# First convolution in float16 parts, its padding on ScalarE and GpSimd, pair loops written out

## What is computed

```python
x = x + L0(gn(x))   # a 3x3 convolution whose weights are mixed for each image
x = x + L1(gn(x))   # 3x3 convolution by groups, quantised weights and sums
x = x + L2(gn(x))   # a two-dimensional cosine transform of each 28x28 plane
x = x + L3(gn(x))   # attention over 784 tokens, 4 heads

def L0(x):
    pooled = mean(x, axis=(2, 3))
    y = (relu(pooled @ fc1_w.T) @ fc2_w.T + fc2_b).reshape(B, 4, 64)
    prob = softmax(y / 4, axis=1)
    agg_w = einsum('bko,koihw->boihw', prob, weight)   # 64x64x3x3 per image
    return conv3x3(x, agg_w)                           # padding 1
```

## Time and profile before

| | us |
|---|---|
| median of 3 runs | 1765.08 (1764.5 to 1770.01) |
| the profiled execution, its own time | 1766.6 |
| its span in the profile | 1763.9 |
| busy: PE / DVE / ACT / POOL | 1597.4 / 1292.2 / 1023.8 / 455.2 |

### The profile page before, as it was taken

How to read it: one execution, slowest core, us unless ns; L and a number is a source line. 1 busy time by engine, 2 the same in 40 slices (tenths; PEclk the granted TensorE clock), 3 DMA queues, 4 the chain that set the end, 5 groups by cost and what they waited for, 6 DMA issues and landing times.

```text
span 1763.9 us, 30283 instructions
## 1 busy us (share of the span) xinstructions
PE 1597.4 (91%) x10848; PEld 730.4 (41%) x10848; DVE 1292.2 (73%) x2666; ACT 1023.8 (58%) x1401; POOL 455.2 (26%) x364
## 2 busy tenths in 40 slices
PE   0699869999686799999999999999999999999997
PEld 0333335555575234444344444444444444444332
DVE  5677557887787687787677777877778778777762
ACT  0000156676132157777677777777777777777676
POOL 0400011110300313234233242333333423333212
PEclk9999989999897689999999999999999999999999
DMA  8122166665000423322333234323332343233300
GB/s 204 32 53 52 31 96 108 108 100 92 1 0 1 64 33 50 50 43 35 52 50 50 44 41 63 49 34 50 51 52 44 40 63 50 34 52 50 52 12 19
DMA packets 71213, 92.82 MB, mean 53 GB/s; under 512 B 23516, under 2 KB 64340, under 8 KB 70960
## 3 DMA queue, kind: packets, MB, share of 16 engines
q1 hardware_dynamic: 67728, 89.59, 31.3%
q0 software_dynamic: 3360, 1.61, 1.3%
HBM read 9.00 MB, written 6.42 MB: 9 GB/s over the span
## 4 chain that ended last, share of the span: by engine, by line
PE 76%; DVE 10%; DMA 5%; ACT 3%; SPq 3%; issue 2%; POOL 1%; DVEq 0%; ACTq 0%
PE ps L1050 19%; PE ps L1040 16%; PE ps L985 14%; PE ps L860 8%; PE ps L884 5%; DVE arena L1430 3%; PE ps L899 3%; DMA arena<-arena 3%; PE ps L1006 2%; ACT arena L678 2%; PE ps L946 2%; DMA x<-x_in 2%; SPq L431 2%; PE ps L1023 1%; PE ps L1014 1%
## 5 line engine op out<-in xcount | busy, mean ns | idle before, releaser
L1430 DVE TENSOR_REDUCE arena<-ps 128x1 f32<-128x392 f32 x1600 | 826.4, 561 | 258.5 <-PE ps L985 246.8
L791 ACT ACTIVATE arena<-ps 112x784 f32<-112x784 f32 x896 | 704.2, 822 | 232.2 <-PE ps L1040 224.9
L985 PE MATMUL ps<-arena 112*128 112x392 bf16 x1536 | 483.8, 341 | 16.2 <-DMA arena<-arena 8.2
L1040 PE MATMUL ps<-arena 114*112 114x392 bf16 x1792 | 443.3, 334 | 6.6 <-ACT arena L791 5.9
L1050 PE MATMUL ps<-arena 112*32 112x392 f32 x3584 | 391.2, 508 | 0.5 <-ACT arena L791 0.5
L985 PEld LDWEIGHTS ps<-arena 112*128 112x128 bf16 x1536 | 149.3, 97 | 367.2 <-DVE arena L1430 301.7
L1040 PEld LDWEIGHTS ps<-arena 114*112 114x112 bf16 x1792 | 228.1, 133 | 107.2 <-ACT arena L791 38.8
L884 PE MATMUL ps<-arena 96*128 96x392 f16 x768 | 142.2, 336 | 22.1 <-DMA arena<-arena 16.6
L678 ACT ACTIVATE arena<-ps,magic,arena 128x784 f32<-128x784 f32 x128 | 128.2, 1005 | 37.0 <-PE ps L884 36.8
L860 PE MATMUL ps<-arena 128*64 128x392 f32 (+1 forms) x768 | 139.7, 506 | 3.9 <-DMA arena<-arena 3.9
L1050 PEld LDWEIGHTS ps<-arena 112*32 112x32 f32 x3584 | 70.7, 108 | 141.8 <-issue 140.0
(11 more groups left out here) (142 smaller groups left out, 1383.7 us busy)
## 6 DMA issues: line engine op xcount, KB each, us to landing
arena<-arena SPq DMA_DIRECT2D x504, 73.5 KB, 2.7
arena<-arena SPq DMA_DIRECT2D x256, 84.2 KB, 2.7
x<-x_in SPq DMA_DIRECT2D x8, 784.0 KB, 21.0
out<-x SPq DMA_DIRECT2D x16, 392.0 KB, 2.9
arena<-arena SPq DMA_DIRECT2D x252, 24.5 KB, 2.4
arena<-arena SPq DMA_DIRECT2D x256, 1.5 KB
arena<-arena SPq DMA_DIRECT2D x16, 225.0 KB, 3.4
arena<-arena SPq DMA_DIRECT2D x16, 224.8 KB, 2.9
```

What stands on the lines that cost most here:

```text
L791: nc.scalar.activation(probs[w % 2][:, 2 * pair:2 * pair + 2, :], two(2 * place, rows=slice(0, TT)), ACT.Exp).then_inc(s_taken, 1)
L985: last = nc.tensor.matmul(ps[:, bank, 0:CH], q[0:ROWS_L, h, it * 128:(it + 1) * 128], k[0:ROWS_L, h, c * CH:(c + 1) * CH], start=True, sto ...
L1040: last = nc.tensor.matmul(ps[0:TT, 2 * place + j, 0:CH], ks[s % 4][0:ROWS_ALL, h, jt * TT:(jt + 1) * TT], qs[s % 4][0:ROWS_ALL, h, c * CH: ...
L1430: nc.vector.tensor_reduce(mx[img % 2][:, c, v:v + 1], scores, AX.X, ALU.max).then_inc(s_mf, 1)
```

## The change

- **Products.** Weights and normalised image are each split into a high and a low float16 part. The weights' two parts lie one below the other on the 128 rows (64 input channels high, 64 low); `pads` holds the image's high and low plane, each on both halves of the partitions. For each of nine taps and each image part (k) there is one product over 128 rows, so all four terms are summed: 18 steps for each half and image, in place of 6. The mixed weights are scaled by the largest weight (`w_max`), taken back when the result is added.
- **Weights.** ACT makes the high part (`agg_high`), POOL the low part (`agg_low`), PE turns them by nine products with a float16 identity, ACT copies all 1152 columns out at once (`take_weights`).
- **Padding.** DVE's `pad` is gone. ACT writes the high plane of both images and a float32 copy `xn0` (`pad`, three instructions), POOL subtracts to get the low planes (`low0`, two instructions of 64 partitions). `pads` has three buffers.
- **Second stage's weights.** POOL's sixteen instructions on them are gone; ACT scales them after pair 1's weights (`scale_w1`, eight instructions), DVE clips and rounds them after pair 3 (`quantise_w1`, two).
- **Start.** The statistics' second half has the maximum of the weights ahead of it; two small steps (`nshift`) and one on `lmax` are added to the chain, and POOL clears its planes at the very start.
- **Loops.** `pair_steps` and DVE's loops become plain repetition over 16 pairs in all three stages, on all engines.

```diff
-        pair_w = [part([128, 3, 128]) for _ in range(2)]
-        last_w = [part([C, 3, 128]) for _ in range(2)]
+        agg_parts = [part([128, 9, 2, C], F16) for _ in range(2)]
+        tap_w = [part([128, 9, 128], F16) for _ in range(2)]
+        ident16 = part([128, 128], F16)
+        w_max = part([128, 1])
+        w_max_inv = part([128, 1])
...
-        pads = [[part([128, PAD]) for _ in range(2)] for _ in range(2)]
+        pads = [[part([128, 2, PAD], F16) for _ in range(2)] for _ in range(3)]
...
-            for p in range(4):
-                step(p, None)
-            with eng.Fori(0, PAIR_LOOP[1]) as i:
-                for j in range(2):
-                    step(4 + j, i)
-            for p in (NP - 2, NP - 1):
+            for p in range(NP):
...
+                first, second = pads[p % 3]
+                sp.wait_ge(s_pad, p + 1)
+                sp.dma_start(first[C:2 * C, :, :], first[0:C, :, :]).then_inc(s_twin[p % 3], 16)
+                sp.dma_start(second[0:C, :, :], second[C:2 * C, :, :]).then_inc(s_twin[p % 3], 16)
...
+            def low0(p):
+                pool.wait_ge(s_xn0, p + 1)
+                for im in range(2):
+                    r = slice(im * C, (im + 1) * C)
+                    inner = [pads[p % 3][im][r, k, 0:HP * WP].rearrange("p (y x) -> p y x", y=HP)[:, 1:1 + H, 1:1 + W]
+                             for k in range(2)]
+                    if im == 1:
+                        pool.wait_ge(s_pad_first, p + 1)
+                    elif p >= 1:
+                        pool.wait_ge(s_agg_parts, p)
+                    nc.gpsimd.tensor_tensor(inner[1], xn0[p % 2][r, :].rearrange("p (y x) -> p y x", y=H),
+                                            inner[0], ALU.subtract).then_inc((s_pad_first, s_pad)[im], 1)
+            def agg_low(p):
+                pool.wait_ge(s_pad, p + 1)
+                pool.wait_ge(s_agg_hi, p + 1)
+                nc.gpsimd.tensor_tensor(agg_parts[p % 2][:, :, 1, :], agg[p % 2][:, :, :], agg_parts[p % 2][:, :, 0, :],
+                                        ALU.subtract).then_inc(s_agg_parts, 1)
...
+            def pad(p):
+                if p >= 3:
+                    act.wait_ge(s_conv, 2 * (p - 2))
+                if p >= 2:
+                    act.wait_ge(s_pad, p - 1)
+                for im in range(2):
+                    r = slice(im * C, (im + 1) * C)
+                    nc.scalar.activation(
+                        pads[p % 3][im][r, 0, 0:HP * WP].rearrange("p (y x) -> p y x", y=HP)[:, 1:1 + H, 1:1 + W],
+                        x[r, p, :].rearrange("p (y x) -> p y x", y=H), ACT.Identity,
+                        bias=nshift[r, p:p + 1], scale=grstd[r, p:p + 1])
+                nc.scalar.activation(xn0[p % 2][:, :], x[:, p, :], ACT.Identity, bias=nshift[:, p:p + 1],
+                                     scale=grstd[:, p:p + 1]).then_inc(s_xn0, 1)
+            def agg_high(p):
+                act.wait_ge(s_agg, p + 1)
+                if p >= 2:
+                    act.wait_ge(s_aggt, p - 1)
+                nc.scalar.activation(agg_parts[p % 2][:, :, 0, :], agg[p % 2][:, :, :], ACT.Copy).then_inc(s_agg_hi, 1)
+            def take_weights(p):
+                act.wait_ge(s_aggt, p + 1)
+                if p >= 2:
+                    act.wait_ge(s_conv, 2 * (p - 1))
+                nc.scalar.activation(tap_w[p % 2].rearrange("p t n -> p (t n)"), weights_psum,
+                                     ACT.Copy).then_inc(s_convw, 1)
+            def scale_w1():
+                act.wait_ge(s_w1, 16)
+                for g in range(NG):
+                    for s, n0 in ((inv_sw, 0), (minus_inv_sw, 64)):
+                        a = w1_raw[:, g, :, n0:n0 + 64]
+                        last = nc.scalar.activation(a, a, ACT.Identity, bias=0.0, scale=s[0:W1_ROWS, g:g + 1])
+                last.then_inc(s_w1_scaled, 1)
             roots(0)
+            act.wait_ge(s_init, 1)
+            act.wait_ge(s_l0v, 1)
+            pad(0)
             act.wait_ge(s_l0v, 3)
             nc.scalar.activation(prob[:, :, :], logit[:, :, :], ACT.Exp).then_inc(s_l0s, 1)
-            def l0(p, i):
-                act.wait_ge(s_aggt, lin(lambda q: q + 1, p, i, 2))
-                if p >= 2:
-                    act.wait_ge(s_conv, lin(lambda q: 2 * (q - 1), p, i, 2))
-                nc.scalar.activation(pair_w[p % 2].rearrange("p y n -> p (y n)"), ps[:, 0, 0:3 * 128], ACT.Copy)
-                nc.scalar.activation(last_w[p % 2].rearrange("p y n -> p (y n)"), ps[0:C, 1, 0:3 * 128],
-                                     ACT.Copy).then_inc(s_convw, 1)
-            pair_steps(l0, act)
+            pad(1)
+            agg_high(0)
+            agg_high(1)
+            take_weights(0)
+            for p in range(NP):
+                if p + 2 < NP:
+                    pad(p + 2)
+                if p + 1 < NP:
+                    take_weights(p + 1)
+                if p == 1:
+                    scale_w1()
+                if p + 2 < NP:
+                    agg_high(p + 2)
...
             def l0_transpose(p, i):
-                pe.wait_ge(s_agg, lin(lambda q: q + 1, p, i, 2))
+                pe.wait_ge(s_agg_parts, p + 1)
                 if p >= 1:
-                    pe.wait_ge(s_convw, lin(lambda q: q, p, i, 2))
-                for y in range(3):
-                    n = slice(y * 128, (y + 1) * 128)
-                    nc.tensor.transpose(ps[:, 0, n],
-                                        agg[p % 2][:, 3 * y:3 * y + 2, :].rearrange("p t i -> p (t i)"), P("ident"))
-                    last = nc.tensor.transpose(ps[0:C, 1, n], agg[p % 2][:, 3 * y + 2, :], P("ident"))
+                    pe.wait_ge(s_convw, p)
+                for t in range(9):
+                    last = nc.tensor.matmul(weights_psum[:, t * 128:(t + 1) * 128],
+                                            agg_parts[p % 2][:, t, :, :].rearrange("p k i -> p (k i)"), ident16[:, :],
+                                            start=True, stop=True)
                 last.then_inc(s_aggt, 1)
             def l0(p, i):
                 if p == 0:
                     l0_transpose(0, None)
                 pe.wait_ge(s_convw, lin(lambda q: q + 1, p, i, 2))
-                pe.wait_ge(s_twin[p % 2], lin(lambda q: 32 * (q // 2 + 1), p, i, 2))
+                pe.wait_ge(s_twin[p % 3], 32 * (p // 3 + 1))
                 for c in range(2):
                     bank = 3 + 2 * (p % 2) + c
                     if p >= 2:
                         pe.wait_ge(s_added, lin(lambda q: 2 * (q - 2) + c + 1, p, i, 2))
-                    for single in range(2):
-                        for y in range(3):
-                            for im in range(2):
-                                rows = slice(0, C if single else 128)
-                                w = (last_w if single else pair_w)[p % 2][:, y, im * C:(im + 1) * C]
-                                at = (y + c * HC) * WP + 2 * single + im
-                                rhs = pads[p % 2][im][rows, at:at + HC * WP].rearrange(
-                                    "p (y x) -> p y x", x=WP)[:, :, 0:W]
-                                last = nc.tensor.matmul(ps[im * C:(im + 1) * C, bank, 0:CH], w, rhs,
-                                                        start=(y == 0 and not single), stop=(y == 2 and single == 1))
+                    for n in range(2 * 9):
+                        (y, dx), k = divmod(n // 2, 3), n % 2
+                        at = (y + c * HC) * WP + dx
+                        for im in range(2):
+                            rhs = pads[p % 3][im][:, k, at:at + HC * WP].rearrange(
+                                "p (y x) -> p y x", x=WP)[:, :, 0:W]
+                            last = nc.tensor.matmul(ps[im * C:(im + 1) * C, bank, 0:CH],
+                                                    tap_w[p % 2][:, n // 2, im * C:(im + 1) * C], rhs,
+                                                    start=(n == 0), stop=(n == 17))
                     last.then_inc(s_conv, 1)
...
+                if q == 2:
+                    dve.wait_ge(s_w0, 16)
+                    link(v.tensor_reduce(w_max[:, :], w0[:, :, :].rearrange("p k n -> p (k n)"), AX.X, ALU.max,
+                                         apply_absolute_value=True))
+                    link(v.tensor_scalar(w_max[:, :], w_max[:, :], 1e-30, None, ALU.max))
+                    link(v.reciprocal(w_max_inv[:, :], w_max[:, :]))
...
+            link(v.tensor_tensor(nshift[:, :], gmean[:, :], grstd[:, :], ALU.mult))
+            v.tensor_scalar(nshift[:, :], nshift[:, :], -1.0, None, ALU.mult)
...
+            link(v.tensor_scalar(lmax[:, :], lmax[:, :], w_max_inv[:, 0:1], None, ALU.mult))
...
+            def quantise_w1():
+                dve.wait_ge(s_w1_scaled, 1)
+                a = w1_raw.rearrange("p g y n -> p (g y n)")
+                link(v.tensor_scalar(a, a, 0.0, QW, ALU.max, ALU.min))
```

(13 more changed lines are left out.)

83 lines of the change are left out of this document (29 added, 54 removed).

## The result

| | before | after |
|---|---|---|
| median of 4 runs, us | 1764.79 (1761.16 to 1770.01) | 1744.1 (1740.62 to 1748.47) |
| ratio, 95% interval | | 0.9885 (0.9865 to 0.9905) |
| span of the profiled execution | 1763.9 | 1746.7 |
| busy: PE / DVE / ACT / POOL | 1597.4 / 1292.2 / 1023.8 / 455.2 | 1556.9 / 1312.5 / 1087.9 / 513.0 |
| first stage's products, from PE's timeline | 62.4 to 213.2 (150.7) | 69.8 to 200.9 (131.1) |

The kernel is 20.7 us faster. The forecast was 40.4 us, 1724.7 us, and its range ended at 1742: the time lies 2 us above it. The forecast of "faster" was right, the size wrong by half.

The account below looks back on a forecast made before the run. PE alone was taken to bound the first stage, 7.31 us a pair in place of 9.31. 32.7 us saved there plus 7.7 from third-stage loops made 40.4 us, giving 1724.7 us; range 1712 to 1742.

Parts of the forecast that it names:

- I take no cost: First stage: POOL and DVE slowing each other adds nothing; PE's 7.31 us a pair still holds, with little room.
- The rival that I gave 0.16: First stage: DVE and POOL shut each other out, about 8.0 us a pair, 11 us more, 1736 us; chance 0.16.
- The range: Whole kernel: 1712 to 1742 us, holding the forecast, shutting out, no loop gain, most of the chain rival and some mixtures.
- The products: First stage on PE: 36 double steps of 0.181 us, 6.51 us a pair; lower end 6.15.
- The transposes: First stage on PE: nine 16-bit products of 128 columns with weight loads, 0.8 us a pair (0.5 to 1.1).
- PE not fed: First stage: 162 PE instructions a pair not sustained; 11.0 us a pair, 59 us more, 1784 us; chance 0.05.
- ACT and POOL: First stage: ACT busy 4.4 us and POOL 4.5 us a pair, both under PE's 7.31.
- The second stage's weights: First stage, after pair 3: `quantise_w1` takes some 2.3 us on DVE with about 1.3 free; counted at 0.3 us.
- The head: Before the first stage's products: first product at 61.5 us against 62.43, 0.9 us less, with 0.15 for disturbance by POOL.
- The third stage: Loops written out: DVE's copies 5.25 us apart throughout, 7.7 us less.
- The second: Second stage, loops written out: nothing to gain, taken as 0, bounds -1 and +3 us.
- The sum: Whole kernel: 32.7 us from the first stage and 7.7 from the loops, 40.4 us less together.

Follow-up runs that it names:

- e5: Kernel after with POOL's `low0` left out but for one pixel set to zero: 1719.71 us, ratio 0.9744.
- e6: Kernel after with each subtraction of `low0` replaced by two memsets, which write and read nothing: 1719.95 us, ratio 0.9752.
- e2: Kernel after with each subtraction of `low0` replaced by two copies with one input each: 1731.48 us, ratio 0.9817.
- e4: Kernel after with both images' planes made in one 128-partition buffer, one ACT cast, one POOL subtraction, four transfers: 1726.90 us, ratio 0.9789.
- e9: Kernel after with the hardware loops put back in the second and third stages: 1746.18 us, ratio 0.9909.
- e11: Repeat run of the kernel after with the hardware loops put back in the second and third stages: 1748.17 us, ratio 0.9907.
- e8: Kernel after with both images' planes in one buffer, the mix's first product on ACT, and first weights taken out earlier: 1720.11 us, ratio 0.9764.
- e1: Kernel after, unchanged, run once more: 1745.45 us, ratio 0.9898.

## Why the prediction was wrong

**The step that failed** is "I take no cost", for POOL and DVE slowing each other. The rival that I gave 0.16 was the truth: it said 8.0 us a pair, measured are 8.27. Its price was put at 11 us against the forecast's 7.31 a pair; against what PE really allows, 6.84, it cost 19.4 us of PE's waiting (e5 and e6 against after: 131.1 - 111.6 = 19.5). The rival's mechanism is what the traces show, its nearness in part luck: its sum put POOL's 4.5 us and the mix into one time, while POOL is busy 12.0 of 20 us and the pair is DVE's 5.8 us with two waits of 1.23.

The reason I gave against it was the earlier trace rows: L1273 was at most 0.11 us longer while POOL was busy without a break. That is so, but what ran beside L1273 there were L517 and L521, GpSimd instructions with one input and a constant, and not the form of `low0`. The L520 that took 2.00 us "beside its mix" ran beside two L1284 and the mix's one-input first product. What the number of inputs has to do with it the runs do not show: e2's copies have one input too, and they shut the multiply-adds out. Why L517 and L521 did not is open.

And the trace before had the signs. The slow L1271 of the earlier trace rows, 0.85 us, ended 0.31 us behind L520's end, as e4's L1332 does behind its subtraction. In the fourth stage stood the very pair of forms, POOL with two inputs and DVE with two. Timeline of POOL and of DVE, kernel before:

```profile
684.58 1.69 POOL L561 TENSOR_TENSOR arena<-arena 128x784 bf16<-128x784 f32 x1
685.76 0.56 DVE L1435 TENSOR_TENSOR arena<-arena 128x25 f32<-128x25 f32 x1
```

L1435 takes 0.19 us at the median; here it took 0.56 and ended 0.04 us behind L561's end. Beside the one-input copy L559 it took 0.34 at 620.00, and ended 0.04 us behind that. They cost almost nothing there, so they stand in no list of costs, but they would have given the rule the larger chance.

**The range** ended at 1742, with the price of the likeliest rivals in the stage alone. It had nothing for the head, where this case's profiles show 5 us of chance in x's arrival and 3 us of contention.

**The products.** 6.51 us forecast, 6.24 measured, 0.173 a double step: nearer to the end L899 gave (0.171) than to L884 (0.181). **The transposes.** 0.8 forecast, 0.60 measured, 0.067 each, near the lower end. The Trainium skill's 81 ns for a load and product of 128 columns (TensorE: Matmul & The Clock Gate, Back-to-back issue gap) is higher than the 67 ns of this stream. Together the period of PE alone was over-sized by 0.47 us, 7.5 us in 16 pairs, which hid part of the other error.

**PE not fed** was wrong: in e5 162 instructions in 6.84 us, 42 ns each, for 112 us without idle time.

**ACT and POOL.** `pad` is three times 1.04 us (forecast 0.86), `take_weights` 1.11 (1.21), `agg_high` 0.69 (0.63): 4.9 us against 4.4, as a sum of durations. `low0` alone is 3.31 us for two (forecast 3.26), so that 64 partitions cost what 128 do, as assumed; `agg_low` 1.27 (1.2). These terms were right. DVE's own work would have fitted too, as e6 shows.

**The second stage's weights** were counted at 0.3 us. `quantise_w1` (L1350, L1351, 0.96 us each) stands in DVE's list, which now is the full one: the pair with it takes 9.81 us in place of 8.27, 1.5 us more. In e5, where DVE has time left, it takes 6.91 in place of 6.84.

**The head.** The first product came at 69.8 us, forecast 61.5. Of the 8.3 us, 5.1 are x's arrival (43.90 against 38.77 us). The repetitions show it between 39.7 and 44.2, so a single profile of before gives it to no better than that. The other 3.2 fit the same contention: POOL's `low0` of the first two pairs and `agg_low` of the first, on which the prediction put 0.15 us. Timeline of DVE and POOL, kernel after:

```profile
56.34 1.52 DVE L1318 TENSOR_TENSOR arena<-arena 128x64 f32<-128x64 f32 x1
...
58.73 0.77 DVE L1323 TENSOR_SCALAR arena<-arena 128x16 f32<-128x16 f32 x1
...
63.35 4.63 DVE L1339 SCALAR_TENSOR_TENSOR arena<-arena 128x576 f32<-128x576 f32 x3
```

```profile
56.19 3.28 POOL L533 TENSOR_TENSOR arena<-arena 64x784 f16<-64x784 f32 x2 [52.32 <-ACT arena L679]
63.74 1.55 POOL L539 TENSOR_TENSOR arena<-arena 128x576 f16<-128x576 f32 x1 [4.27 <-ACT arena L686]
65.44 4.01 POOL L533 TENSOR_TENSOR arena<-arena 64x784 f16<-64x784 f32 x2
```

L1318 takes 1.52 us beside L533, where the same shape (L1324) takes 0.23 after it; L1323, of 16 columns, takes 0.77, where L1314 of the same shape takes 0.24; and the second pair's multiply-adds 4.63 in place of 2.5, beside L539 and then L533: 1.3, 0.5 and 2.1 us, more than the 3.2 that they have to explain. The prediction took POOL off the head (its clearing and quantising) and did not see that it put two other instructions back at the same place.

**The third stage** was right: 7.7 us forecast, 8.5 measured, and at the place given, DVE's steps inside the loop; whether register work is the reason was not taken apart. **The second** was forecast at 0 (-1 to +3): +1.9 in the profile after and +1.7 in its repetition, -0.6 and -0.5 with the loops alone, +0.6 and +0.9 in e9 and e11. So about 1 us of it comes from writing out in the changed kernel and 1 from the changed first stage; which step does it is open.

**The sum**, by spans: forecast 40.4, measured 17.2. The difference of 23.2 us is start 8.3, first stage 131.1 - 119.0 = 12.1, second 1.9, third -0.8, fourth 1.8 (within its own spread), to 0.1 us.

## What to carry to other kernels

Work moved from a full engine to an idle one is not free if both read SBUF at the same time: before VectorE's work is laid beside a GpSimd instruction that reads there, look whether any row of the trace shows just that pair of forms, and if none does, count the GpSimd instruction's whole length on VectorE. Do not read sharing from durations alone: compare the ends. If one engine's long instructions all end the same time behind the other's, they take turns, and a small instruction that costs nothing shows it as well as a large one. Fewer, wider GpSimd instructions cost half (64 partitions take as long as 128), and what remains is best laid beside a VectorE instruction whose engine has idle time. And a repetition of both kernels' profiles before a term is taken from the head or from a stage with rare transfer waits shows how far one profile can be trusted: here 4 us at the head and 9 us in the fourth stage.

## What the runs showed of the hardware

- Two inputs on VectorE against two on GpSimd: they take turns by whole instructions. 0.82 becomes 2.04 us (L1339), ending 0.61 us behind the GpSimd instruction; that one's 1.62 becomes 2.04 (e8, L533), ending 1.47 behind VectorE's. GpSimd copying with one input: turns as well, 0.82 becomes 1.27 and 0.83 becomes 1.25 (e2). GpSimd only writing: 0.82 stays (e6). GpSimd with one input and a constant: at most 0.11 us on the multiply-adds (L517, L521 in the kernel before).
- A one-input VectorE instruction of 0.51 us took 1.84 when it started 0.08 us behind a two-input GpSimd instruction of 1.62 us (e4, L1332), and up to 1.12 beside memsets (e6, L1338): one input did not protect it. The expectation of e4 had looked only at the multiply-adds.
- The hardware loop costs DVE 0.6 to 1.0 us a pair, 7.8 us in the third stage (e9, e11 against after). Whether that is its semaphore values made from the register, or the loop otherwise, was not taken apart.
- A wait of TensorE of 2.1 us for a transfer was followed by a granted clock of 0.68 and 0.81 over the next two stretches of 10 us (after); one of 2.04 us by 0.83 and 1.00 (e1); one of 0.40 us by 1.00 (e9).
